# Tokens of the joint experts turned by VectorE in 32x32 blocks, by way of a scratch in memory, instead of by TensorE

## The chip, the cores and the metric

The kernel runs on one core of one Trainium2 chip. The metric is device time in microseconds, the median of several executions. Before the change: 745.49 us, median of 3 runs (743.95 to 746.71).

## What is computed

Two batches of 2048 rows of 512 numbers pass through two layers of attention and mixing and through a quantised layer (the first phase of the kernel), and then through a layer of 16 experts. Each expert picks its 128 best tokens in each batch, takes them through three matrix products and adds the result, weighted, back to those rows:

```python
logits = einsum('bsd,de->bse', x, Wg) + bg
probs = softmax(logits, axis=-2)                     # over the tokens
vals, idx = top_k(transpose(probs, (0, 2, 1)), 128)  # per batch and expert
xe = x[bidx, idx]                                    # 128 rows of 512
h = relu(xe @ w1[e] + b1[e]); h = relu(h @ w2[e] + b2[e])
out = scatter_add(x, idx, (h @ w3[e] + b3[e]) * vals)
```

## The kernel before

The first phase works on 32 tiles of 128 rows and takes the span up to some 418 us. It leaves the normalised rows in memory (`xn4`). Experts 0 to 3 of batch 0 ("early", `tok_e`) are computed while the other experts' tokens are still being chosen, up to some 466 us. The last stage, from about 475 us on, has twelve *joint* experts (e = 0 to 11, for experts 4 to 15), each for both batches at once, and four *single* ones (s = 0 to 3: experts 0 to 3 of batch 1), which are woven into the joint experts 1, 4, 7 and 9 (`SINGLE`). A joint product is made of three passes, since numbers are split into a high part (`_h`) and the rest (`_l`). A single one takes one pass.

How the tokens of a joint expert came to PE: POOL gathers 128 rows of each batch with an indirect DMA (`gather`, `tok`, a token on each partition). PE turns them in eight 128x128 transposes (`tokens`, line 1318) into two PSUM banks, so that the features lie on the partitions: chunk c holds the features 128c to 128c+127. ACT copies the high part to `tokT_h` (`token_hi`), DVE subtracts it from the bank into `tokT_l` (`token_lo`). For a single expert there are four transposes (`single_tokens`, line 361 in `four_transposes`) and a copy by ACT (`single_copy`).

The order of an iteration e on each engine is written out by hand:
- PE: `single_tokens`, `hidden(e, 0)`, `single_first`, `tokens(e + 1)`, `outputs(e - 1)`, `single_second`, `hidden(e, 1)`, `single_outputs` (those of a single expert only where one is woven in).
- ACT: `split_hi(3e + 1)`, `single_copy`, `relu(e, 0, .)` twice, `single_relu`, `token_hi(e + 1)`, `split_hi(3e + 2)`, `single_relu`, `split_hi(3e + 3)`, `relu(e, 1, .)` twice.
- DVE: `split_lo(3e + 1)`, `hidden_lo(e, 0, .)` twice, `token_lo(e + 1)`, `split_lo(3e + 2)`, `weighted(e - 1, 0)`, `split_lo(3e + 3)`, `weighted(e - 1, 1)`, `hidden_lo(e, 1, .)` twice.
- POOL: `gather(e + 2)`, then the adds of e - 1 to the output.
- SP: `load_raw(i)`, 1 MB of weights into one of three buffers, waits until the split of load i - 3 is done. `load_single` brings a single expert's weights, 1 MB each.

Each engine takes its own list in order. A weight passes from `w_raw` through `split_hi` (ACT) and `split_lo` (DVE) before PE uses it. Load 3e - 1 holds the first weights of expert e, 3e + 1 the second, 3e + 3 the third. Line 1973 is the subtraction of all `_lo` steps, line 1496 the copy of all `_hi` steps, line 354 the products in three passes, line 994 and line 1423 those of a single pass. Line 2124 is an operation of the first phase that writes every fourth word (`lg_t`); line 1251 loads every second column of a tile into PE.

Of the kernel before, what the change touches and what calls it, by code (L numbers as in the profile page):

```python
# [35 lines left out]
P = 128  # L36
# [12 lines left out]
def build(nc, io):  # L49
# [36 lines left out]
        p_ev a_ev p_sv a_sv s_gather  # L86
# [12 lines left out]
    sem_tok = [[ctx.enter_context(nc.semaphore(f"tok_in{i}{b}")) for b in range(B)] for i in range(2)]  # L99
# [195 lines left out]
    tok_h, tok_l = place("tokT_h", [P, C, B * P], F32R), place("tokT_l", [P, C, B * P], F32R)  # L295
    tokT_s, h1_s = place("single_tokT", [P, D]), place("single_h1", [P, D])
# [4 lines left out]
    for i in range(RAW, WR):  # L301
        w_h.append(place(f"w_h{i}", [P, C, D], F32R))
    pos = place("pos", [P, TOP], U32)
# [6 lines left out]
    es = place("es", [HEADS, GB])  # L310
    y_s = place("single_y", [P, D])
    bias_s = place("single_bias", [P, FIRST])
    assert top[0] <= at_cd + 16 * KB, (top[0], at_cd + 16 * KB)
# [44 lines left out]
    def four_transposes(pe, bank, src):  # L358

        for c in range(C):  # L360
            last = pe.transpose(bank[:, c * P:(c + 1) * P], src[:, c * P:(c + 1) * P], ident[:, :])  # L361
        return last

# [213 lines left out]
    def _(sp):  # L577
# [48 lines left out]
        def load_early(i):  # L626
# [3 lines left out]
            sp.dma_start(w_e[RING[i % 5]][:, :, :], chunked(io.w[layer][e])).then_inc(sem_early[i % 5], 16)  # L630
# [57 lines left out]
        def load_raw(i):  # L688
# [4 lines left out]
            sp.dma_start(w_raw[i % RAW][:, :, :], chunked(io.w[layer][FIRST + e])).then_inc(sem_raw[i % RAW], 16)  # L693

        def load_single(s, layer):
# [4 lines left out]
            else:  # L700
                at, was = divmod(i - 4, 3)
                sp.wait_ge(sm.p_sv, 4 * at + was + 2)
            sp.dma_start(w_e[i % 4][:, :, :], chunked(io.w[layer][s])).then_inc(sem_early[i % 4], 16)
# [39 lines left out]
    def _(pe):  # L743
# [240 lines left out]
        def early_tokens(e):  # L984
# [3 lines left out]
            four_transposes(pe, bank, tok_e[e]).then_inc(sm.p_ev, 1)  # L988
# [318 lines left out]
        def tokens(e):  # L1307
            for b in range(B):
                pe.wait_ge(sem_tok[e % 2][b], 16 * (e // 2 + 1))
                if e == 0:  # L1310
                    pe.wait_ge(sm.k_pos, 2)
                else:
                    pe.wait_ge(sm.d_tlo, B * (e - 1) + b + 2)
                    if b == 1 and e - 1 in SINGLE:
                        pe.wait_ge(sm.a_sv, 4 * SINGLE[e - 1] + 1)
                for c in range(C):
                    bank = token_bank(e, b, c)
                    last = pe.transpose(bank[:, c * P:(c + 1) * P], tok[e % 2][:, b, c * P:(c + 1) * P], ident[:, :])  # L1318
                last.then_inc(sm.p_tok, 1)

        def hidden(e, layer):
# [3 lines left out]
            if layer == 0:  # L1325
                pe.wait_ge(sm.d_tlo, 2 if e == 0 else B * (e + 1) + 1)
# [4 lines left out]
            for pair in range(2):  # L1331
# [3 lines left out]
                if layer == 1 and e in SINGLE:  # L1335
                    pe.wait_ge(sm.a_sv, 4 * SINGLE[e] + 2 + pair)
# [40 lines left out]
        def outputs(e):  # L1377
# [3 lines left out]
            for b in range(B):  # L1381
# [3 lines left out]
                if b == 1 and e in SINGLE:  # L1385
                    pe.wait_ge(sm.a_sv, 4 * SINGLE[e] + 4)
# [10 lines left out]
        def single_tokens(s, u):  # L1397

            pe.wait_ge(sm.s_gather, 16 * (s + 1))
            pe.wait_ge(sm.d_tlo, B * u + 3)  # L1400
            four_transposes(pe, ps_tok[1], tok_s).then_inc(sm.p_sv, 1)

        def single_first(s, u):
# [3 lines left out]
            pe.wait_ge(sm.a_sv, 4 * s + 1)  # L1407
            early_layer(ps_hid[2], w, tokT_s, range(C)).then_inc(sm.p_sv, 1)

        def single_second(s, u):  # L1410
# [3 lines left out]
            pe.wait_ge(sm.a_sv, 4 * s + 2)  # L1414
            early_layer(ps_hid[3], w, h1_s, range(C)).then_inc(sm.p_sv, 1)

        def single_outputs(s, u):
# [3 lines left out]
            pe.wait_ge(sm.a_sv, 4 * s + 3)  # L1421
# [40 lines left out]
        tokens(0)  # L1462
        keep_warm(3, wh, ps_y[0])
        for e in range(JOINT):
            if e in SINGLE:
                single_tokens(SINGLE[e], e)
# [3 lines left out]
            if e + 1 < JOINT:  # L1470
                tokens(e + 1)
# [14 lines left out]
    def _(act):  # L1486
# [1451 lines left out]
```

## Time and profile before

| | |
|---|---|
| median of 3 runs | 745.49 us (743.95 to 746.71) |
| span of the profiled execution | 743.2 us |
| PE, busy | 716.2 us (96%) |
| DVE, busy | 521.6 us (70%) |
| ACT, busy | 401.9 us (54%) |
| POOL, busy | 420.4 us (57%) |
| chain that ended last | PE 84%, issue 6%, DMA 4%, DVE 3% |
| moved by DMA | 118.04 MB, mean 159 GB/s |

The profile is of one execution. The span runs from its first to its last instruction, and the measured time is 2.3 us longer. PE is TensorE's products and PEld its weight loads, DVE is VectorE, ACT ScalarE, POOL GpSimd, and SP the engine that issues most of the DMAs. The chain is the work that ended last, followed back from the last instruction to what released each step. The joint stage is the part from 475 to 734 us.

### The profile page before, as it was taken

Reading aid. Unit: us, or ns where it says so; the run is one execution under the profiler, and the core shown is the slowest. Engines: PE = TensorE matmul, PEld = TensorE weight load, DVE = VectorE, ACT = ScalarE, POOL = GpSimd, SP = SyncE. Lnnn points to the kernel's source line nnn. Section 1 sums busy time; section 2 is a strip of 40 time slices with the busy share of each in tenths; the row PEclk is TensorE's granted clock in tenths of the full one; section 3 lists DMA queues with packets and bytes.
Section 4 is the critical chain, followed back from the end, with each engine's and each line's share of the span. In section 5 each row is a group of like instructions: output and inputs, shape, how many; then the busy total and the mean of one; then the engine's idle time right before and its main releaser. Section 6 shows DMA issues by size and latency. Waiting matters only on the chain.

```text
span 743.2 us, 12766 instructions
## 1 busy us (share of the span) xinstructions
PE 716.2 (96%) x4513; PEld 624.9 (84%) x4513; DVE 521.6 (70%) x978; ACT 401.9 (54%) x680; POOL 420.4 (57%) x621
## 2 busy tenths in 40 slices
PE   6999999999999999999999799999999999999994
PEld 5765888888888888888888778798999899899894
DVE  5786789889888888876896697464663565463561
ACT  5755444444544545868668334364664656464641
POOL 2825788888888887786788622503521443340132
PEclk9999999999999999999999899999999999999998
DMA  9610121221222213111117898696796698895534
GB/s 317 256 30 15 43 86 62 88 86 58 88 79 82 71 58 108 52 60 44 49 45 264 322 396 279 149 391 186 222 370 185 185 330 293 289 266 167 142 86 58
DMA packets 61671, 118.04 MB, mean 159 GB/s; under 512 B 6056, under 2 KB 7464, under 8 KB 61608
## 3 DMA queue, kind: packets, MB, share of 16 engines
q1 hardware_dynamic: 54312, 100.44, 38.7%
q0 software_dynamic: 7296, 16.78, 10.3%
q8 instruction: 37, 0.61, 0.3%
q14 instruction: 26, 0.21, 0.1%
HBM read 91.76 MB, written 25.21 MB: 157 GB/s over the span
## 4 chain that ended last, share of the span: by engine, by line
PE 84%; issue 6%; DMA 4%; DVE 3%; ACT 2%; POOL 1%; POOLq 0%; SPq 0%; DVEq 0%; ACTq 0%
PE bank L354 39%; PE banks L354 9%; PE bank L361 6%; PE bank L994 6%; PE banks L861 4%; PE banks L867 4%; DMA out<-y,ids 3%; PE banks L871 2%; PE banks L994 2%; PE banks L872 2%; PE banks L1423 1%; PE banks L1028 1%; PE bank L1318 1%; PE bank L1041 1%; DMA out<-x 1%
## 5 line engine op out<-in xcount | busy, mean ns | idle before, releaser
L2844 POOL DMA_INDIRECT out<-y,ids x24 | 46.1, 1922 | 157.4 <-DVE y L2555 155.5
L1973 DVE TENSOR_TENSOR w_l<-w_raw,w_h 128x2048 fp32r<-128x2048 f32 x35 | 80.1, 2291 | 63.2 <-ACT w_h L1496 49.4
L1961 DVE BATCH_NORM_STATS2 bn<-x 128x6 f32<-128x512 f32 x113 | 77.7, 688 | 8.2 <-DMA x<-x 5.4
L1496 ACT ACTIVATE w_h<-w_raw 128x2048 fp32r<-128x2048 f32 x36 | 68.5, 1918 | 7.2 <-DMA w_raw<-w 7.2
L1892 ACT ACTIVATE h<-bank,b 128x512 f32<-128x512 f32 x48 | 33.0, 688 | 62.5 <-PE bank L354 57.8
L1973 DVE TENSOR_TENSOR hT_l<-h,hT_h 128x512 fp32r<-128x512 f32 x48 | 33.0, 689 | 39.8 <-ACT hT_h L1898 37.7
L354 PE MATMUL bank<-tokT_h,w_h 128*128 128x256 f32 x188 | 55.1, 293 | 0.0
L2607 POOL TENSOR_SCALAR rstd<-mean_var 128x1 f32<-128x1 f32 x108 | 25.7, 238 | 50.9 <-DVE mean_var L1966 42.6
L354 PE MATMUL bank<-tokT_h,w_l 128*128 128x256 f32 x188 | 53.2, 283 | 0.0
L354 PE MATMUL bank<-tokT_l,w_h 128*128 128x256 f32 x188 | 53.2, 283 | 0.0
L354 PE MATMUL bank<-wf_h,xdT_h 128*128 128x512 f32 x128 | 52.6, 411 | 0.0
L354 PE MATMUL bank<-wf_h,xdT_l 128*128 128x512 f32 x128 | 50.3, 393 | 0.0
L354 PE MATMUL bank<-hT_h,w_h 128*128 128x256 f32 x176 | 50.1, 285 | 0.0
L354 PE MATMUL bank<-wf_l,xdT_h 128*128 128x512 f32 x128 | 50.0, 390 | 0.0
L354 PE MATMUL bank<-hT_l,w_h 128*128 128x256 f32 x176 | 49.8, 283 | 0.0
L354 PE MATMUL bank<-hT_h,w_l 128*128 128x256 f32 x176 | 49.8, 283 | 0.0
L1650 ACT ACTIVATE q<-bank,bq 128x512 f32<-128x512 f32 x32 | 22.0, 688 | 45.0 <-PE bank L354 44.5
L2687 POOL TENSOR_TENSOR x<-x,mix_bias 128x512 f32<-128x512 f32 x32 | 41.3, 1292 | 1.9 <-PE bank L361 1.8
L2625 POOL TENSOR_TENSOR qT_l<-q,qT_h 128x512 fp32r<-128x512 f32 x32 | 41.4, 1295 | 0.7 <-ACT qT_h L1652 0.7
L2723 POOL TENSOR_TENSOR x<-x,ffn_bias 128x512 f32<-128x512 f32 x32 | 41.8, 1305 | 0.0
L1492 ACT ACTIVATE xn<-x,rstd 128x512 f32<-128x512 f32 x32 | 26.1, 816 | 24.4 <-POOL rstd L2622 20.8
L1973 DVE TENSOR_TENSOR xdT_l<-bank,xdT_h 128x512 fp32r<-128x512 f32 x32 | 22.0, 689 | 23.7 <-ACT xdT_h L1496 23.4
(419 smaller groups left out, 2380.1 us busy)
## 6 DMA issues: line engine op xcount, KB each, us to landing
w_raw<-w SPq DMA_DIRECT2D x36, 1024.0 KB
early_w<-w SPq DMA_DIRECT2D x24, 1024.0 KB, 10.0
x<-x SPq DMA_DIRECT2D x32, 256.0 KB, 2.7
out<-x SPq DMA_DIRECT2D x32, 256.0 KB, 2.0
xn<-xn SPq DMA_DIRECT2D x32, 256.0 KB
mask<-mask_t SPq DMA_DIRECT2D x8, 256.0 KB, 3.4
slot_all<-slots SPq DMA_DIRECT2D x4, 512.0 KB, 7.8
stage<-wk SPq DMA_DIRECT2D x1, 1024.0 KB, 7.7
```

The lines of the kernel that those rows point to most:

```text
L354: last = pe.matmul(out, a, b, start=(n == 0), stop=(n == 3 * len(pairs) - 1))
L361: last = pe.transpose(bank[:, c * P:(c + 1) * P], src[:, c * P:(c + 1) * P], ident[:, :])
L861: last = pe.matmul(both_halves[:, a, 0:WIDE], xh[:, d, :], wc_h[:, d, a, :], start=(d == 0), stop=(d == C - 1))
L994: last = pe.matmul(bank[:, c * P:(c + 1) * P], w[:, d, c * P:(c + 1) * P], x[:, d * P:(d + 1) * P], start=(d == 0), stop=(d == C - 1))
L1496: act.activation(dst, src, ACT.Copy).then_inc(sem, 1)
L1892: act.activation(h32[n % 2][:, :], ps_hid[n % 4][:, :], ACT.Relu, bias=bias)
L1961: dve.bn_stats(bn6[which][:, j % 2, :], src[:, :]).then_inc(sem_bn[which], 1)
L1973: dve.tensor_tensor(dst, src, hi_part, ALU.subtract).then_inc(sem, 1)
L2625: pool.tensor_tensor(dst, src, hi_part, ALU.subtract).then_inc(sem, 1)
L2687: pool.tensor_tensor(x2[j % 2][:, :], x2[j % 2][:, :], cbias[:, batch(j), :], ALU.add).then_inc(sm.g_x2b, 1)
L2723: pool.tensor_tensor(x1_of(k)[:, :], x1_of(k)[:, :], fbias[:, :], ALU.add).then_inc(sm.g_x1b, 1)
L2844: pool.indirect_dma_start(out=out_rows, out_offset=bass.IndirectOffsetOnAxis(ap=ids[:, r:r + 1], axis=0), in_=y[e % 2][b][:, :], in_offset ...
```

## The change

The gathered rows of joint experts 1 to 11 and of all single experts are no longer turned by PE. SP stores them to a scratch in memory (`parts`, `single`) in pieces of 128 numbers: the scratch holds first the first quarter of every token, then the second quarter, and so on. SP then loads it back with 512 contiguous numbers to a partition, so that partition 32q + n holds quarter q of the tokens 4n to 4n + 3. DVE transposes this in 32x32 blocks (`turn_blocks`), reading and writing every fourth number. After it, partition p holds the features 4p to 4p + 3, where it held p, 128 + p, 256 + p and 384 + p before. The first layers' weights are loaded to match: "(p c) n" for "(c p) n", which makes four rows of a weight one contiguous run of 8 KB to a partition. The early tokens and those of joint expert 0 are still transposed by PE, reading every fourth column (`four_row_transposes`, `first_tokens`).

`tok_raw`, which the turns write, lies in the place of `tok_l`: a turn waits until `hidden(e - 1, 0)` has ended, and `token_lo` works in place. Both batches' high parts are made by one copy on ACT, and the rests by one subtraction on DVE. The turns stand where `token_lo` stood; `token_hi` and `token_lo` come later in the lists, behind the next weight's split. The store and the load stand on SP behind every third `load_raw`, each with its waits. `gather(e)` on POOL waits for the store of expert e - 2.

```diff
+        def turn_blocks(eng, out, rows):
+            return eng.transpose(out.rearrange("p c (k t) -> p t c k", k=QBLK),
+                                 rows.rearrange("p (t k c) -> p t c k", t=P // QBLK, c=C))
+        def expert_weights(layer, e):
+            w = io.w[layer][e]
+            return w.rearrange("(p c) n -> p c n", c=C) if layer == 0 else chunked(w)
...
+        def store_parts(e):
+            sp.wait_ge(sem_tok[e % 2], 32 * (e // 2) + (32 if e % 2 else 16))
+            if e >= 2:
+                sp.wait_ge(sm.q_in, 16 * (e - 1))
+            for b in range(B):
+                sp.dma_start(io.parts[b].rearrange("(q p f) -> p q f", p=P, f=P),
+                             tok[e % 2][:, b, :].rearrange("p (q f) -> p q f", f=P)).then_inc(sm.q_out, 16)
+        def load_parts(e):
+            sp.wait_ge(sm.q_out, 16 * B * e)
+            if e == 1:
+                sp.wait_ge(sm.k_pos, 2)
+            if e >= 2:
+                sp.wait_ge(sm.d_tr, B * (e - 1))
+            sp.dma_start(tok_parts[:, :, :], io.parts.rearrange("b (p f) -> p b f", p=P)).then_inc(sm.q_in, 16)
...
         for b in range(B):
-            sp.wait_ge(sem_tok[0][b], 16)
+            sp.wait_ge(sem_tok_first[b], 16)
+        store_parts(1)
+        store_single(0)
+        load_parts(1)
+        load_single_parts(0)
         for i in range(RAW + 1, len(order)):
             load_raw(i)
+            e = i // 3 + 1
+            if i % 3 == 1 and e < JOINT:
+                store_parts(e)
+                if e in SINGLE:
+                    store_single(SINGLE[e])
+                load_parts(e)
+                if e in SINGLE:
+                    load_single_parts(SINGLE[e])
...
         for e in range(JOINT):
-            if e in SINGLE:
-                single_tokens(SINGLE[e], e)
             hidden(e, 0)
             if e in SINGLE:
                 single_first(SINGLE[e], e)
-            if e + 1 < JOINT:
-                tokens(e + 1)
...
         def token_hi(e):
-            for b in range(B):
-                act.wait_ge(sm.p_tok, B * e + b + 1)
-                act.wait_ge(sm.p_h, max(0, 4 * (e - 1) + 2))
-                for part in token_parts(e, b):
-                    hi(sm.a_thi, tok_h[:, part, b * P:(b + 1) * P], in4(token_bank(e, b, part.start))[:, part, :])
+
+            act.wait_ge(sm.d_tr, B * e)
+            hi(sm.a_thi, tok_h[:, :, :], tok_raw[:, :, :])
...
+        def turn_tokens(e):
+
+            dve.wait_ge(sm.p_h, 4 * e - 2)
+            for b in range(B):
+                dve.wait_ge(sm.q_in, 16 * e)
+                turn_blocks(dve, tok_raw[:, :, b * P:(b + 1) * P], tok_parts[:, b, :]).then_inc(sm.d_tr, 1)
+        def token_lo(e):
+
+            dve.wait_ge(sm.a_thi, e + 3)
+            lo(sm.d_tlo, tok_l[:, :, :], tok_raw[:, :, :], tok_h[:, :, :])
...
             if e + 1 < JOINT:
-                token_lo(e + 1)
+                turn_tokens(e + 1)
+            if e + 1 in SINGLE:
+                turn_single(SINGLE[e + 1])
             for n in range(2):
                 if nxt < len(order):
                     split_lo(nxt)
                     nxt += 1
                 if e >= 1:
                     weighted(e - 1, n)
+                if n == 0 and e + 1 < JOINT:
+                    token_lo(e + 1)
...
         def gather(e):
-            if e >= 2:
-                pool.wait_ge(sm.p_tok, B * (e - 1))
+            if e == 2:
+                pool.wait_ge(sm.p_tok, B)
+            if e >= 3:
+                pool.wait_ge(sm.q_out, 16 * B * (e - 2))
```

## Rows read from the trace of the kernel before

**Rows 1.** The page: the span, and PE's busy time.

```profile
span 743.2 us, 12766 instructions
PE 716.2 (96%) x4513; PEld 624.9 (84%) x4513; DVE 521.6 (70%) x978; ACT 401.9 (54%) x680; POOL 420.4 (57%) x621
```

**Rows 2.** Busy time by stretches; last columns: granted clock, DMA share, GB/s.

```profile
core 0: us, PE busy (x) PEld busy (x) DVE busy (x) ACT busy (x) POOL busy (x), PEclk, DMA share, GB/s
516.78:534.62 17.84, 17.84 (x131) 16.89 (x130) 11.41 (x10) 10.96 (x12) 9.05 (x5) 1.00 0.76 217
534.62:552.50 17.88, 17.88 (x131) 16.89 (x130) 11.42 (x10) 11.44 (x13) 4.17 (x4) 1.00 1.04 356
415.00:420.00 5.00, 2.21 (x11) 2.22 (x12) 3.43 (x11) 3.88 (x7) 2.77 (x7) 0.60 0.69 268
475.00:706.00 231.00, 230.88 (x1648) 213.24 (x1649) 127.78 (x117) 129.76 (x153) 72.32 (x47) 1.00 0.80 250
```

**Rows 3.** The chain that ended last, in time: start, length, what.

```profile
487.75 0.44 PE bank L361 x4
488.19 5.76 PE bank L354 x48
...
522.54 0.87 PE bank L1318 x8
```

**Rows 4.** Groups of instructions: count, busy us, mean ns, idle before.

```profile
L1973 DVE TENSOR_TENSOR w_l<-w_raw,w_h 128x2048 fp32r<-128x2048 f32 x35 | 80.1, 2291 | 63.2 <-ACT w_h L1496 49.4 <-issue 13.8
L1496 ACT ACTIVATE w_h<-w_raw 128x2048 fp32r<-128x2048 f32 x36 | 68.5, 1918 | 7.2 <-DMA w_raw<-w 7.2
L1973 DVE TENSOR_TENSOR tokT_l<-bank,tokT_h 128x512 fp32r<-128x512 f32 x23 | 14.8, 685 | 15.9 <-ACT tokT_h L1496 15.9
L1496 ACT ACTIVATE tokT_h<-bank 128x512 fp32r<-128x512 f32 x23 | 12.5, 600 | 5.9 <-issue 5.9
L1318 PEld LDWEIGHTS bank<-ident,tok 128*128 128x128 f32 x94 | 10.6, 141 | 0.6 <-DMA tok<-xn,ids 0.5
L1251 PEld LDWEIGHTS bank<-pack,ident 128*64 128x64 f32 x16 | 1.3, 138 | 0.2
```

**Rows 5.** DVE in time: a strided write (L2124) and a dense one.

```profile
362.58 0.27 DVE L2124 TENSOR_TENSOR lg_t<-lg,rstd_all 128x64 f32<-128x64 f32 x1
...
390.30 0.22 DVE L2109 TENSOR_TENSOR lg<-lg,lg_sum 128x64 f32<-128x64 f32 x1
```

**Rows 6.** DVE in time, in the iteration of e=2.

```profile
523.87 0.69 DVE L1973 TENSOR_TENSOR hT_l<-h,hT_h 128x512 fp32r<-128x512 f32 x1 [1.54 <-ACT hT_h L1898]
...
528.86 0.81 DVE L2555 TENSOR_SCALAR y<-banks,b,vals 128x512 f32<-128x512 f32 x1
```

**Rows 7.** DMA: packets, MB, share in 487.75 to 505; in 475 to 706; issues.

```profile
q1 hardware_dynamic: 2799, 5.54, 85.2%
...
q0 software_dynamic: 5279, 12.45, 22.2%
...
x<-x SPq DMA_DIRECT2D x32, 256.0 KB, 2.7
out<-x SPq DMA_DIRECT2D x32, 256.0 KB, 2.0
...
later<-later SPq DMA_DIRECT2D x1, 64.0 KB, 2.2
...
slots<-slot_rows SPq DMA_DIRECT2D x1, 16.0 KB, 1.8
```

**Rows 8.** SP's issues, and ACT, in time, in the iteration of e=3.

```profile
531.94 8.55 SPq L693 DMA_DIRECT2D w_raw<-w  x2
...
547.63 1.91 ACT L1496 ACTIVATE w_h<-w_raw 128x2048 fp32r<-128x2048 f32 x1 [3.17 <-DMA w_raw<-w]
```

**Rows 9.** SP, POOL and DVE in time, at the start of the joint stage.

```profile
446.75 31.21 SPq L693 DMA_DIRECT2D w_raw<-w  x3
...
472.47 0.94 POOL L2833 DMA_INDIRECT tok<-xn,ids  x1 [0.30 <-issue]
...
482.44 0.69 DVE L1973 TENSOR_TENSOR hT_l<-h,hT_h 128x512 fp32r<-128x512 f32 x1 [2.13 <-ACT hT_h L1898]
483.05 1.28 DVE L1973 TENSOR_TENSOR tokT_l<-bank,tokT_h 128x512 fp32r<-128x512 f32 x2
```

More of the change, by code:

```diff
@@ L98, in build @@
     sem_raw = [ctx.enter_context(nc.semaphore(f"raw_in{i}")) for i in range(RAW)]
[L99 removed]
+    sem_tok = [ctx.enter_context(nc.semaphore(f"tok_in{i}")) for i in range(2)]
+    sem_tok_first = (sem_tok[0], ctx.enter_context(nc.semaphore("tok_in_first1")))
     sem_cut = [ctx.enter_context(nc.semaphore(f"cut_in{i}")) for i in range(2)]
@@ L302, in build @@
         w_h.append(place(f"w_h{i}", [P, C, D], F32R))
+    at_parts = top[0]
+    tok_parts = place("tok_parts", [P, B, D], at=at_parts)
     pos = place("pos", [P, TOP], U32)
@@ L362, in four_transposes, with of_chunk, four_row_transposes @@
         return last
+    def of_chunk(rows, c):
+        return rows[:, c::C]
+    def four_row_transposes(pe, bank, rows):
+        for c in range(C):
+            last = pe.transpose(bank[:, c * P:(c + 1) * P], of_chunk(rows, c), ident[:, :])
+        return last
+    def turn_blocks(eng, out, rows):
[4 more added lines that the diff above has]
+        return w.rearrange("(p c) n -> p c n", c=C) if layer == 0 else chunked(w)
     def blocks(t):
@@ L692, in load_raw @@
                 lo_done(sp, i - RAW)
-            sp.dma_start(w_raw[i % RAW][:, :, :], chunked(io.w[layer][FIRST + e])).then_inc(sem_raw[i % RAW], 16)
+            sp.dma_start(w_raw[i % RAW][:, :, :], expert_weights(layer, FIRST + e)).then_inc(sem_raw[i % RAW], 16)
         def load_single(s, layer):
@@ L1304, in _, with first_tokens @@
         pe.transpose(ps[0][:, 0:HEADS], top_v[:, :], ident[0:HEADS, 0:HEADS]).then_inc(sm.k_tr, 1)
-        def tokens(e):
+        def first_tokens():
             for b in range(B):
[L1309 to L1315, printed above, removed]
+                pe.wait_ge(sem_tok_first[b], 16)
+                pe.wait_ge(sm.k_pos, 2)
                 for c in range(C):
-                    bank = token_bank(e, b, c)
-                    last = pe.transpose(bank[:, c * P:(c + 1) * P], tok[e % 2][:, b, c * P:(c + 1) * P], ident[:, :])
+                    bank = token_bank(0, b, c)
+                    last = pe.transpose(bank[:, c * P:(c + 1) * P], of_chunk(tok[0][:, b, :], c), ident[:, :])
                 last.then_inc(sm.p_tok, 1)
@@ L2532, in split_lo, with first_token_lo, turn_single @@
             lo(sm.d_w, w_l[i % WR][:, :, :], w_raw[i % RAW][:, :, :], w_h[i % WR][:, :, :])
-        def token_lo(e):
+        def first_token_lo():
             for b in range(B):
                 t = slice(b * P, (b + 1) * P)
-                for i, part in enumerate(token_parts(e, b)):
-                    dve.wait_ge(sm.a_thi, B * e + b + 1 + (i if e == 0 else 1))
-                    lo(sm.d_tlo, tok_l[:, part, t], in4(token_bank(e, b, part.start))[:, part, :], tok_h[:, part, t])
+                for i, part in enumerate(token_parts(0, b)):
+                    dve.wait_ge(sm.a_thi, b + 1 + i)
+                    lo(sm.d_tlo, tok_l[:, part, t], in4(token_bank(0, b, part.start))[:, part, :], tok_h[:, part, t])
+        def turn_tokens(e):
+            dve.wait_ge(sm.p_h, 4 * e - 2)
+            for b in range(B):
+                dve.wait_ge(sm.q_in, 16 * e)
[3 more added lines that the diff above has]
+            lo(sm.d_tlo, tok_l[:, :, :], tok_raw[:, :, :], tok_h[:, :, :])
+        def turn_single(s):
+            dve.wait_ge(sm.qs_in, 16 * (s + 1))
+            if s >= 1:
+                dve.wait_ge(sm.p_sv, 3 * s - 2)
+            turn_blocks(dve, tokT_s[:, :].rearrange("p (c t) -> p c t", c=C), h1_s[:, :]).then_inc(sm.d_ts, 1)
         def hidden_lo(e, layer, pair):
@@ L2556, in weighted @@
                               ALU.add, ALU.mult).then_inc(sm.d_y, 1)
-        token_lo(0)
+        first_token_lo()
         split_lo(1)
@@ L2574, in _ @@
                     weighted(e - 1, n)
+                if n == 0 and e + 1 < JOINT:
+                    token_lo(e + 1)
             hidden_lo(e, 1, 0)
@@ L2933 @@
     io["cut"] = nc.dram_tensor("cut", (4 * 2048, 1), F32, kind="Internal").ap()
+    io["parts"] = nc.dram_tensor("parts", (2, 128 * 512), F32, kind="Internal").ap()
+    io["single"] = nc.dram_tensor("single", (128 * 512,), F32, kind="Internal").ap()
     io["slots"] = nc.dram_tensor("slots", (4 * 2048,), BF16, kind="Internal").ap()
```

71 lines of the change are left out of this document (39 added, 32 removed).

## The prediction

> **What bounds the kernel now.** I read the page first: TensorE is busy 96% of the span [rows 1]. Then the table of stretches, cut at the starts of the joint experts' first layers: from 475 to 706 us PE is busy for 230.88 of 231 us at clock 1.00, and DVE, ACT and POOL for 55%, 56% and 31% [rows 2]. Then the chain of work that ended last: from 475 to 684 us it is PE without a gap, so a microsecond taken from PE there ends the kernel a microsecond earlier as long as nothing else is late. In that chain stand the transposes that the change removes: 0.87 us for the eight of a joint expert (11 such pieces) and 0.44 us for the four of a single one (4 pieces) [rows 3]. A hidden layer is 5.76 us. The reserve that matters is the DMA engines': mean share 0.80 from 475 to 706, but 1.04 in the iteration of e=3 [rows 2].
>
> **What is removed.** 11 x 0.87 + 4 x 0.44 = 11.3 us of PE, all on the chain. ACT loses two copies of some 0.6 from PSUM for each expert and gains one of 128x1024, half of the 1.92 of a 128x2048 and a little, say 1.0; DVE's two subtractions of 0.69 become one of 128x1024, half of 2.29, 1.2 us [rows 4]. These two changes are even.
>
> **The turns.** New on DVE are two 32x32-block transposes of 128x512 for each expert, one for a single. The trace has none. A DVE pass over 128x512 takes 0.69 [rows 4]. Read and written data here lie 16 bytes apart. Such a write is in the trace: 128x64 with every fourth word takes 0.27 where a dense one takes 0.22 [rows 5], 0.05 for 64 elements, so 0.4 for 512. Bounds: 0.69, and 16 blocks each as an instruction of its own. For the latter, 128x64 at 0.22 bounds a block of 32 columns, call it 0.19: 3.0 us. I take 1.0, the dense pass with most of the strided write, since it is nearest to that row. The Trainium skill, "SBUF — State Buffer", section "Door 1: The DMA port swizzle", says that an access that crosses to another 16-byte line pays a penalty, with fp32 free up to four elements. These turns cross on every access, reading and writing. The row agrees for the write, with 0.05 us in 64. By the rule the read pays as well, 1.4 instead of 1.0 a turn, and the sum would be worse by about 1 us, at the start only.
>
> **Do the turns hide in a plain iteration?** Take e=2, from 516.78. hidden_lo(2, 0, 1) ends 7.8 us after the start, and then came both subtractions [rows 6]. Now: turns to 9.8, split_lo 12.1, weighted (0.81) 12.9, token_lo 14.1. PE wants the tokens at 17.84 - 0.87 = 17.0. Reserve 2.9 us, so no cost; it is gone when a turn takes about 2.5. In a single's iteration there is much more. DVE's sum goes from 11.4 [rows 2] by 2.0 + 1.2 - 1.4 to 13.2 of 17.0.
>
> **PE's strided reads.** The 16 early and 8 first token transposes now load every fourth column. The load of a tile with every second column (L1251) took 138 ns, a dense one 141 [rows 4]. I take nothing; doubled loads would cost 24 x 0.14 = 3.4 us, some on the chain. That is the upper bound.
>
> **The DMAs.** A hardware packet of 2 KB cost 0.852 x 16 x 17.25 / 2799 = 84 ns, so a 1 MB weight load is 2.7 us of all engines [rows 7]. An expert's load of parts is 256 such: 1.3 us. Its store is 1024 packets of 512 B, bounded by a quarter of 84 ns and by 84 ns: 1.3 to 5.4 us. A 64 KB load made of 512 B rows landed in 2.2 us where 16 KB took 1.8 [rows 7], so a packet is near the lower end; I take 27 ns, 1.7 us. Together 3.1 for an expert and 1.5 for a single: 11 x 3.1 + 4 x 1.5 = 40 us of DMA, on top of 0.80 x 231 = 185. Until the weights end that is 225 of some 223 us: full on average, though the share can go to 1.05. The first layers' weights come with 8 KB runs instead of 2 KB; the bytes are the same and no such load is in the trace; I take nothing, and a tenth of 14 such loads, 4 us of DMA either way, as bounds.
>
> **The waits on SP.** SP now stands at the store until the gather has landed, and at load_parts until the store has. Behind it stand load_raw(3k+5), load_single and load_raw(3k+6), and behind those ACT's splits. The store joins a hardware queue behind weights already issued. How long that queue gets: load_raw(12) issued at 531.94 and split at 547.63, after 3.17 us of waiting [rows 8]. POOL's transfers take 0.222 x 231 / 46 = 1.1 us of all engines each [rows 7]; four loads, two adds and two gathers make 4 x 2.7 + 4 x 1.1 = 15.2 of these 15.7 us, so the queue works in order and is full. Now for k=2, from its start T: load 10 at T+5; store done at T+12.4; load_parts, then load 11 at T+13.4 instead of T+12.1; singles; load 12 at T+17; the load of parts in front. Load 12 then lands some 32 us after T, 15 after the start of e=3, ACT's split ends at 16.8 and relu(3, 1, 0) at 18.1. PE wants it at 17.0 + 5.8 = 22.8. So 4 to 5 us of reserve, no cost. The same holds at k=5; at k=7 the long iteration drains the queue. POOL's gather(e) now waits for the store of e-2 instead of its transposes; the stores are done before POOL comes to it, except at the start.
>
> **The start.** Here nothing is ahead. The second gather of expert 5 was issued at 472.47, and I let it land at 476.2. Two stores issued to 477.2, done at 480.5 (1.7 of data, 1.3 fixed, which is an out store's 2.0 less 0.7 of data, and 0.3 beside an early add); load_parts 480.5 to 484.0 (1.3 of data, 2.0 fixed, which is an x load's 2.7 less 0.7, and its issue), load_single_parts 484.6 [rows 7]. Before, DVE ended hidden_lo at 483.13 and subtracted at once [rows 9]. Now: two turns to 486.0, turn_single 487.0, split_lo(2) 489.3, token_lo(1) 490.5. hidden(1, 0) began at 488.19 [rows 3] and now begins at 490.6: 2.4 us later, though PE is free at 487.5. A PE idle of 3 us could lower the clock: after 5 us without work it was granted 0.60 in 415 to 420 [rows 2]. That would add up to 2 us; I leave it to the range. SP then issues load_raw(4) at 481.5 (477.96 before) [rows 9], and load_single(0, 0) at 489.3, since load_parts(2) waits for a store behind load_raw(4), landing about 495, before PE wants it at 496.4.
>
> **Sum.** +2.4 at the start of e=1. From there ten token pieces and three single ones fall away: -8.7 - 1.3. Net -7.6 at the end of the stage. The last expert and its adds are as before. The span of the profiled execution is 743.2 [rows 1], the median 745.49, so 2.3 lie around it: 743.2 - 7.6 + 2.3 = 737.9.
>
> **Rivals.**
> A, all hidden: the parts arrive as early as the old transposes and hidden(1, 0) starts at 487.5. Then 11.3 less 0.6 (DVE's hidden_lo ends at 483.13 and PE must wait for it without the eight transposes): 745.5 - 10.7 = 734.8. Against it: the start's four steps in a row.
> B, slower side: the DMA engines become the bound. Each store followed by its load on SP empties the hardware queue for the fixed time of 1.3 to 2.0 us [rows 7]. With 225 us of work in 223 and 10 such gaps of 2 us, 22 us are too much. Load 12 has 5 us of reserve and a single's long iteration gives some back, say 12 in all, so some 10 us come out as PE stalls at e=4, 7 and 9: 737.9 + 10 = 748. It decides once load 12 lands more than 5 us later than above, that is with 512 B packets above some 45 ns or with gaps in every iteration. For it: share 1.04 [rows 2] and the wait [rows 8]. Against it: in most iterations SP waits for a split anyway.
> C, also slower: a turn costs 3.0. Token_lo ends at 18.1 in a plain iteration instead of 17.0, 7 times 1.1, and the start is later by 6: 737.9 + 7.7 + 6 = 752.
> D, no effect: the freed PE time goes to another wait of the same size, such as single_outputs on weighted: 745.5. Against it: PE has no idle in the stage now, and no removed transpose stands between single_second and single_outputs.
>
> **Chances.** Forecast 0.52, A 0.10, B 0.21, C 0.07, D 0.10. The range takes A and B with the store's and the clock's bounds: 734 to 748.5. The likeliest case's own range is 735 to 741.5. A measurement tells 0.5% (3.7 us) from no change. Faster than 741.8: forecast, A: 0.62. Within: D, half of B: 0.21. Slower than 749.2: C and the worse half of B: 0.17.
>
> **What would show it.** PE records of L1318 only 8, of L361 on single tiles none. A PE gap of about 3 us near 488, ending with token_lo. Transposes on DVE near 1.0. Share of the DMA engines above 0.9 from 490 to 690. ACT waiting for w_raw near e=3 and 6, with no PE gap behind it; a PE gap at single_first or single_outputs speaks for B, at hidden(e, 0) in plain iterations for C.

## The result, and the profile after

The changed kernel takes 754.33 us, median of 4 runs (751.87 to 754.78), where the kernel before takes 745.63 (4 runs, 743.95 to 746.71): ratio 1.0115, 95% interval 1.0095 to 1.0135. It is slower by 1.15%, and outside the range forecast (734 to 748.5), where the forecast was 737.9, faster.

From the page of the changed kernel (span; engines; shares of the chain that ended last):

```profile
span 752.8 us, 12590 instructions
PE 712.1 (95%) x4409; PEld 618.1 (82%) x4409; DVE 544.7 (72%) x993; ACT 399.4 (53%) x665; POOL 425.4 (57%) x621
...
PE 65%; DMA 14%; issue 11%; DVE 5%; ACT 2%; POOL 2%; SPq 1%; POOLq 0%; DVEq 0%; ACTq 0%
```

The 104 matmuls are gone (4513 to 4409 [rows 1]), but PE's busy time fell by 4.1 us and not by 11.3, and PE is 65% of the chain instead of 84%; DMA is 14% of it instead of 4%. The table of stretches tells why (columns as in [rows 2]):

```profile
475.00:706.00 231.00, 216.42 (x1484) 196.62 (x1485) 141.46 (x123) 119.76 (x131) 76.52 (x46) 0.97 0.93 300
...
488.00:492.00 4.00, 0.00 (x0) 0.00 (x0) 3.92 (x3) 4.00 (x5) 0.00 (x0) 0.88 0.97 321
492.00:496.00 4.00, 3.23 (x15) 3.26 (x16) 4.00 (x5) 2.86 (x3) 0.00 (x0) 0.50 0.40 110
...
584.00:588.00 4.00, 2.38 (x4) 1.13 (x5) 2.72 (x4) 0.48 (x1) 1.98 (x3) 0.82 0.89 251
588.00:592.00 4.00, 4.00 (x15) 2.26 (x14) 0.00 (x0) 0.97 (x2) 2.81 (x3) 0.75 1.03 311
```

Between 475 and 706 us PE now stands idle for 14.6 us (0.12 before), and the mean clock is 0.97. PE idles in three places only; the timeline of PE names them (in brackets the idle time and what ended it):

```profile
483.13 0.39 PE L1428 MATMUL bank<-hT_h,w_h 128*128 128x256 f32 x1 [0.65 <-DVE hT_l L2025]
492.77 0.55 PE L359 MATMUL bank<-tokT_h,w_h 128*128 128x256 f32 x1 [5.07 <-DVE tokT_l L2025]
...
580.08 0.36 PE L359 MATMUL bank<-hT_h,w_h 128*128 128x256 f32 x1 [1.91 <-ACT single_h L1962]
585.62 5.37 PE L1482 MATMUL banks<-early_w,single_h 128*128 128x512 f32 x8 [2.45 <-issue]
...
648.22 0.36 PE L359 MATMUL bank<-hT_h,w_h 128*128 128x256 f32 x1 [2.01 <-ACT single_h L1962]
653.76 2.69 PE L1482 MATMUL banks<-early_w,single_h 128*128 128x512 f32 x4 [2.44 <-issue]
```

**The account.** At the start: 0.65 + 5.07 idle, and then `hidden(1, 0)` takes 8.21 us (chain, below) instead of 5.76, since the clock was granted at 0.50, the lower of its two levels, in 492 to 496: 8.2 us in all. In e=4: 1.91 + 2.45 idle, and `single_outputs` takes 5.37 instead of 3.67 (its length where the clock is full, as in the experiment with 2 KB runs): 6.1 us. The same in e=7: 6.1 us. Together 20.4 against 11.3 saved, +9.1; PE's last product ends 9.8 us later than before, so 0.7 are not assigned. (`hidden(0, 0)` begins at 475.06 where it began at 475.12, so these 9.8 us all arise in the joint stage.) No iteration between has a gap, and e=9 has none.

The first chain of the changed kernel, at the start (start, length, what):

```profile
476.56 4.67 DMA parts<-tok
...
482.61 5.45 DMA single_h<-single
...
488.08 1.16 DVE single_tokT L381
489.24 2.14 DVE w_l L2025
491.38 1.15 DVE tokT_l L2025
...
492.77 8.21 PE bank L359 x48
```

Store, load, turn, split and subtraction stand in a row, and in the row forecast; what was wrong is their length. And the second, which ends in e=4:

```profile
543.89 11.05 DMA tok<-xn,ids
...
555.37 8.94 DMA parts<-tok
...
565.29 11.19 DMA w_raw<-w
...
576.50 0.03 ACT w_h L1551
...
578.32 0.96 ACT tokT_h L1551
579.28 0.66 ACT single_h L1962
...
580.08 3.10 PE bank L359 x24
583.17 2.45 issue
585.62 5.37 PE banks L1482 x8
```

Read from below. `single_outputs` (585.62) waits for `weighted(3, 1)` on DVE, which ends at 585.5; it stands in DVE's list behind two weight splits, and the first of them began only at 578.45, after 8.02 us of waiting for ACT's split of the same weight:

```profile
584.71 0.81 DVE L2626 TENSOR_SCALAR y<-banks,b,vals 128x512 f32<-128x512 f32 x1
```

And `hidden(4, 1)` waits for a single expert's hidden values (`single_h`) on ACT. ACT makes them at 579.3 because in its list `split_hi(14)` stands ahead, and this weight landed at 576.5. It landed so late since SP issued it at 565.29, behind `load_parts(5)`, which waits for the store of expert 5, 9 us long; and the store had waited for its gather, 11 us long. So SP stood still twice. The timelines of SP and ACT show the same (from 475 to 740 us ACT waited twice for a weight before, 6.8 us in all, the longest 3.6; now eight times, 44.7 us, the longest 9.6):

```profile
554.96 0.92 SPq L736 DMA_DIRECT2D parts<-tok  x2
564.33 0.36 SPq L746 DMA_DIRECT2D tok_parts<-parts  x1
...
565.29 2.39 SPq L718 DMA_DIRECT2D w_raw<-w  x3
...
576.50 1.91 ACT L1551 ACTIVATE w_h<-w_raw 128x2048 fp32r<-128x2048 f32 x1 [8.71 <-DMA w_raw<-w]
...
ACT w_h L1551 <- DMA w_raw<-w: 44.7, 8, 9.6
```

### The profile page after: what moved, and what is told of

It reads as the page before. It is cut to its first block, busy times and chain, and to the rows that moved or that the text cites. A ratio compares the mean times of both kernels' runs of the same rounds, so it can differ in the third digit from the quotient of the medians.

```text
span 752.8 us, 12590 instructions
## 1 busy us (share of the span) xinstructions
PE 712.1 (95%) x4409; PEld 618.1 (82%) x4409; DVE 544.7 (72%) x993; ACT 399.4 (53%) x665; POOL 425.4 (57%) x621
## 2 busy tenths in 40 slices
DMA packets 71286, 131.66 MB, mean 175 GB/s; under 512 B 6712, under 2 KB 21432, under 8 KB 68664
## 4 chain that ended last, share of the span: by engine, by line
PE 65%; DMA 14%; issue 11%; DVE 5%; ACT 2%; POOL 2%; SPq 1%; POOLq 0%; DVEq 0%; ACTq 0%
PE bank L359 31%; PE bank L366 6%; PE banks L359 5%; PE banks L931 4%; PE banks L937 3%; DMA parts<-tok 3%; DMA w_raw<-w 3%; PE bank L1064 3%; DMA out<-y,ids 3%; DMA tok<-xn,ids 3%; PE banks L941 2%; PE banks L1482 2%; PE banks L942 2%; PE banks L1064 1%; DVE w_l L2025 1%
## 5 line engine op out<-in xcount | busy, mean ns | idle before, releaser
L2921 POOL DMA_INDIRECT out<-y,ids x24 | 48.9, 2036 | 153.8 <-DVE y L2626 152.8
L1551 ACT ACTIVATE w_h<-w_raw 128x2048 fp32r<-128x2048 f32 x36 | 68.8, 1911 | 44.7 <-DMA w_raw<-w 44.7
L359 PEld LDWEIGHTS bank<-tokT_h,w_h 128*128 128x128 f32 x188 | 37.2, 198 | 6.2 <-issue 6.2
```

The lines of the kernel that those rows point to most:

```text
L359: last = pe.matmul(out, a, b, start=(n == 0), stop=(n == 3 * len(pairs) - 1))
L1551: act.activation(dst, src, ACT.Copy).then_inc(sem, 1)
L2921: pool.indirect_dma_start(out=out_rows, out_offset=bass.IndirectOffsetOnAxis(ap=ids[:, r:r + 1], axis=0), in_=y[e % 2][b][:, :], in_offset ...
```

## The experiments

Every run is given as its median, its ratio to the kernel before on the same chip, and the 95% interval. In the profiled executions `hidden(0, 0)`, the start of the joint stage, begins anywhere from 472.6 to 475.9 us, though hardly anything ahead of it differs; so I also compare the stage itself, from there to the end of PE's last product: 258.8 us before, 268.6 in the changed kernel. Three runs (22 products, the single expert's turn behind `token_lo`, every turn twice) were made on another chip than the kernels with which they are compared; the kernel before took 745.0 us there and 745.2 here. My theory W was now: SP's two waits (for the gather and for the store) delay the weights, and the start pays for its chain. Against it: D, the DMA engines are simply full, so that any kernel with this traffic is late; and S, the new 8 KB runs of the first weights are slow.

**The waits without the store's result, then without either.** The first takes the load's wait for the store away, by reading rows that have long been in memory; the second also stores a tile that is always there, so SP doesn't wait for the gather either.

```diff
-            sp.wait_ge(sm.q_out, 16 * B * e)
-            sp.dma_start(tok_parts[:, :, :], io.parts.rearrange("b (p f) -> p b f", p=P))...
+            sp.dma_start(tok_parts[:, :, :], io.xn4[0:B * P, :].rearrange("(b p) f -> p b f", b=B))...
```

> The changed kernel, but load_parts and load_single_parts read fixed rows of xn4 (the same bytes in the same 2 KB pieces), so SP no longer stands there until the store has landed. Left out: the experts then work on wrong tokens. The stores stay, and SP still waits for the gather before a store. Theory W (SP stands at these waits, the weight loads behind it are issued late, and PE waits for them at e=4 and e=7): the start shortens from a gap of 5.1 us and 2.4 us at half clock to a gap of about 2, since the parts are there when DVE is free, and most of the 6 us at each of e=4 and e=7 go: 754.3 - 5.5 - 6 to 12 = 737 to 743. Theory D (the DMA engines cannot carry the extra 12 MB, whoever waits): the traffic is the same, so the 12 us at e=4 and e=7 stay: about 749.

> As the run before, and the stores send a constant tile, so SP waits neither for the gather nor for the store: all the extra traffic, none of the waits of SP on it. Left out: the same as in the run before. Theory W: no gaps at e=4 and e=7, 736 to 739, and faster than the run before by as much as the gather's wait costs. Theory D: 12 us of gaps stay, about 749.

Measured: 740.60 us, 0.9938 (0.9921 to 0.9955), and 737.66 us, 0.9908 (0.9885 to 0.9932). Both move the same 131.66 MB as the changed kernel. The traffic of the second, by stretch (DMA share and GB/s at the end), is denser than the changed kernel's (0.92, 298 from 475 to 700); below it the same stretch of the first:

```profile
475.00:700.00 225.00, 221.49 (x1558) 203.40 (x1558) 150.89 (x130) 129.56 (x140) 83.75 (x47) 1.00 0.95 317
```

```profile
475.00:700.00 225.00, 220.02 (x1530) 202.13 (x1529) 147.05 (x128) 125.40 (x137) 83.34 (x47) 0.98 0.95 315
```

PE's gaps at e=4 and e=7 are gone in both. D falls: the engines carry this traffic at 317 GB/s without a stall. Without the wait for the store the kernel is 13.7 us faster; without the wait for the gather 2.9 more, and these lie at the start (a gap of 4.33 us and a `hidden(1, 0)` of 8.51 in the first; gaps of 1.54 and 1.98, and 5.99, in the second). The total of the first lay in its range, but not for all the reasons expected: the start was to shorten to a gap of about 2 us, and it hardly did. The second stands at the 737.9 of the forecast, and for the forecast's reasons: the transposes saved, a start some 2 us late, no cost from SP (its joint stage is 7.4 us shorter than before, forecast 7.6; this profile is of the fastest of its four runs, 735.1). So most of what the forecast lacked is the price of SP's waits.

**2 KB runs.** The joint experts' first weights are loaded in two DMAs of every second row, which makes runs of 2 KB again.

```diff
-            sp.dma_start(w_raw[i % RAW][:, :, :], expert_weights(layer, FIRST + e))...
+            for part in ((slice(0, C, 2), slice(1, C, 2)) if i % RAW == 2 else (slice(0, C),)):
+                sp.dma_start(w_raw[i % RAW][:, part, :], expert_weights(layer, FIRST + e)[:, part, :])...
```

> The changed kernel with the joint experts' first weights loaded in two transfers of every second row, so that a run is 2 KB again and not 8 KB; the result is the same. Theory S (packets of 8 KB hold back the software queue, so the gather of expert 9 lands 11 us after its issue and all behind it is late): the gather lands in about 5 us, the gaps at e=4 and e=7 fall by half or more, 745 to 749. If the size of a run does nothing: 754 within 2.

Measured: 752.24 us, 1.0103 (1.0086 to 1.0119), an interval that overlaps the changed kernel's; the joint stage is 0.6 us shorter, 268.0. S falls: the gather of expert 5 landed after 9.8 us, not 5, and the store after it took 9.9. The gaps stand where they stood (1.01 + 2.43 in e=4, 3.43 + 0.94 in e=7, and 1.03 and 1.19 elsewhere), with 1.5 us of lower clock in `hidden(7, 1)` instead of `single_outputs`.

**Expert 1 and the first single expert turned by PE, as before.** The diff puts `second_tokens` and `first_single_tokens` on PE, and starts the stores with expert 2.

```diff
-        store_parts(1)
-        store_single(0)
-        load_parts(1)
-        load_single_parts(0)
...
         for e in range(JOINT):
+            if e == 1:
+                first_single_tokens()
             hidden(e, 0)
+            if e == 0:
+                second_tokens()
```

> The changed kernel, but joint expert 1 and single expert 0 are still transposed by PE, as before the change; the scratch serves from joint expert 2 on. The start costs 5.1 us of gap, 0.7 of another and 2.4 of low clock in the changed kernel. Theory: these go and 1.3 us of transposes come back, so 754.3 - 7 = 747.3, with the gaps at e=4 and e=7 as they are. If the lateness at e=4 comes from the late start (the queue of loads that is already behind at e=1), it goes too: about 741.

Measured: 747.58 us, 1.0040 (1.0025 to 1.0055). The total falls by 6.7 us, with 1.3 us of PE given back, so about 8.1 gross where the account says 8.2. Part of this agreement is chance: the profile also has less idle time at e=4 and e=7, and gaps of 1.47 and 0.48 us and 1.5 us of lower clock in `hidden(7, 1)` that the changed kernel doesn't have. The gaps at e=4 (0.84 + 2.45, and 5.37 us of `single_outputs`) and e=7 (2.03 + 0.93) remain, so the two losses are separate.

**The load one weight later, with each start.** Only the place of `load_parts` and `load_single_parts` on SP changes: behind the next `load_raw`.

```diff
             if i % 3 == 1 and e < JOINT:
                 store_parts(e)
                 if e in SINGLE:
                     store_single(SINGLE[e])
+            if i % 3 == 2 and (i + 1) // 3 < JOINT:
+                e = (i + 1) // 3
                 load_parts(e)
```

> The changed kernel with one move in SP's order: the loads of an expert's quarters (and of a single token's) stand one weight load later than their stores, so that SP passes its wait for the store with the next weights already issued. In the changed kernel SP waited for the store of expert 5 from 555.4 to 564.3 us and issued the weights behind it at 565.3, which landed at 576.5. Theory W (the wait for the store, one expert's weights late, is what stops PE at e=4 and e=7): those weights go out some 9 us earlier, the four gaps of 1.91, 2.44, 2.01 and 2.44 us vanish, and with them the 1.7 us of single_outputs at the lower clock, twice: 754.3 - 8.8 - 3.4 = 742. The start is untouched. Theory L (the chain gather, store, load, turn is itself too long for an iteration of 18 us): the parts of expert 5 now land some 10 us later, VectorE's turn waits for them, and with it its splits; the gaps go to hidden(e,0): 752 to 757. Theory G (it is the wait for the gather, ahead of the store, which this kernel keeps): about half of the gain, 748.

> Both cures at once: expert 1 and the first single token are turned by PE as before the change, and the later loads go one weight load behind their stores. With expert 1 by PE the kernel took 747.6 us, with gaps of 0.84 and 2.45 us and 1.7 us of lower clock at e=4 and of 2.03 and 0.93 us at e=7. Theory W: these go, 747.6 - 6.2 - 1.7 = 739.7. Theory L: the gaps move to hidden(e,0), 747 to 751.

Measured: 741.62 us, 0.9956 (0.9940 to 0.9973), and with the old start 734.60 us, 0.9866 (0.9848 to 0.9883). The gaps at e=4 and e=7 are gone with either start, and here the stores and loads carry the true rows, so L and G fall too: the chain is not too long, and the wait for the gather, which both keep, costs nothing there by itself. SP's timeline in the second:

```profile
563.17 0.92 SPq L736 DMA_DIRECT2D parts<-tok  x2
565.67 0.34 SPq L718 DMA_DIRECT2D w_raw<-w  x1
568.74 0.36 SPq L746 DMA_DIRECT2D tok_parts<-parts  x1
...
475.00:706.00 231.00, 231.00 (x1642) 213.30 (x1641) 154.20 (x134) 134.35 (x147) 82.34 (x49) 1.00 0.96 309
```

The last line is its table of stretches: PE has no idle time at all, at full clock, with the DMA engines at 0.96. The weight is issued while the store is still on its way, and ACT waits for weights 12.6 us instead of 44.7. PE ends its work at 723.36, 10.5 us before the kernel before. Of these 0.6 lie ahead of the joint stage; the stage is 9.9 us shorter, and that is the PE work removed, ten token pieces of 0.87 and three of 0.44, 10.0. This version is faster than both kernels, by 1.3% than the one before. I had expected 739.7 and not 734.6: with it went the gaps of 1.47 and 0.48 us and the 1.5 us of lower clock named above, 3.4 of these 5.1 us, where I had added up only the gaps at e=4 and e=7; another 0.6 lies ahead of the stage, and 1.1 is not assigned.

**Stores and loads on ACT's queue.** On top of the old start.

```diff
             relu(e, 0, 0)
+            if 1 <= e < JOINT - 1:
+                load_parts(e + 1)
...
             relu(e, 1, 1)
+            if e + 2 < JOINT:
+                store_parts(e + 2)
```

> As the kernel with expert 1 turned by PE (747.6 us), and the stores and loads of the quarters are issued on ACT's queue instead of SP's: the store of expert e+2 behind the last relu of expert e, the load of expert e+1 behind the first relu of expert e, each where what it waits for has landed long before. SP then waits for no token. Theory W: SP issues its weights as before the change, the gaps at e=4 and e=7 go: 747.6 - 6.2 - 1.7 = 739.7, and a little less if ACT's queue takes the parts' packets out of the order of the weights, 737 to 740; faster than the kernel before. Rival (ACT is the late engine in these iterations and pays for the issues, some 0.1 to 0.4 us each for 3 or 4 of them an iteration, or waits for a gather that took 11 us): 742 to 748.

Measured: 775.93 us, 1.0434 (1.0392 to 1.0476), much slower, and outside both ranges expected. The chain of the profiled execution (769.0 us) says what I had overlooked:

```profile
512.59 10.98 DMA parts<-tok
...
523.58 7.77 DMA tok_parts<-parts
...
531.45 2.19 DVE tokT_raw L381 x2
...
542.58 9.91 DMA tok_parts<-parts
```

SP no longer waits (ACT's wait for weights is down to 0.4 us), but the load for expert e + 1 is now issued only in iteration e, in which DVE has to turn it, and takes 8 to 10 us. So DVE waits for parts 35.0 us in nine times, ACT waits 36.2 us for DVE's turns, and PE stands for 2.9 to 4.9 us at each of five `hidden(e, 0)`, four times for a `relu` that ACT reaches late. ACT's queue also stood for the store itself, twice, 13.0 us. Two things follow. The store takes 11 us on a queue of its own too (512.59 to 523.56): what makes it slow is not, or not only, its place behind weights in SP's queue, as I had thought. (Both queues use the same 16 DMA engines, SP's 51.7% of their time from 475 to 706 us and ACT's 14.8%; whether the weights delay the store there, no run shows.) And the place of the load in the order matters as much as the wait that goes with it.

**The idle time and the clock.** Products of the identity with itself fill the start's gap on PE: 15 on the changed kernel, then 22 on the one with later loads.

```diff
         for e in range(JOINT):
+            if e == 1:
+                for _ in range(15):
+                    pe.matmul(ps_y[0][:, 0:P], ident[:, :], ident[:, :], start=True, stop=True)
             hidden(e, 0)
```

> The changed kernel with 15 products of the identity by itself (128x128, about 0.28 us each, 4.2 us) put on PE ahead of hidden(1,0), where it stood idle for 5.07 us and then took 8.21 us for work that took 5.8 us before. Their result is overwritten. Theory C (the slow hidden(1,0) is the clock, which was granted at half after the idle time): PE is busy in the gap, hidden(1,0) takes 5.8 to 6.2 us, the total is 2.2 us shorter, 752.1. Rival (hidden(1,0) is slow for another reason, its operands arriving piece by piece from ACT and DVE): it takes 8.2 us again and the total is the same, 754.3.

> On top of the later loads (741.6 us), 22 products of the identity by itself ahead of hidden(1,0), 0.234 us apart, 5.1 of the 5.44 us in which PE stood idle there. 15 of them left 1.95 us idle, and hidden(1,0) still took 7.47 us with a granted clock below 1. Theory C (the clock falls for the idle time): with the gap all but full hidden(1,0) takes 5.8 us, 2.3 us less, 739.3. Rival (the products of the identity are not what keeps the clock, or the slow product has another cause): 741.6.

Measured: 751.65 us, 1.0091 (1.0065 to 1.0118), against 754.33; and 739.44 us, 0.9927 (0.9911 to 0.9944), against 741.62. The chains, with 15 products first, then with 22 (L1528 are the products of the identity, two records for each):

```profile
493.83 7.48 PE bank L359 x48
```

```profile
487.49 4.91 PE banks L1528 x44
492.40 5.76 PE bank L359 x48
```

Fifteen left 1.95 us idle, and `hidden(1, 0)` still ran partly at the lower clock (7.48, 0.7 less than without them). The total fell by 2.7, with runs from 747.6 to 755.8. The 2 us beyond that 0.7 are not from the start: in this profile e=4 (0.83 + 2.44 idle) and e=7 (3.45 + 1.03, and 1.4 of lower clock in `hidden(7, 1)`) cost 9.2 us instead of 12.2, though nothing there was changed; with 0.5 at the start that is the 3.5 us by which its joint stage is shorter (265.1). So the price of e=4 and e=7 differs from one execution to another, and this run alone settles nothing. Twenty-two left nothing, and it takes 5.76: 2.2 us off the total, as expected. So at the start the fall of the clock comes from the idle time, and is worth 2.2 to 2.4 us on top of it.

**The single expert's turn behind `token_lo`,** on the version with later loads.

```diff
-            if e + 1 in SINGLE:
-                turn_single(SINGLE[e + 1])
             for n in range(2):
...
                 if n == 0 and e + 1 < JOINT:
                     token_lo(e + 1)
+                if n == 0 and e + 1 in SINGLE:
+                    turn_single(SINGLE[e + 1])
```

> On top of the later loads (741.6 us), VectorE turns a single token's block behind token_lo instead of ahead of the weights' split and token_lo. At the start the single's turn held VectorE for 1.10 us on the way to token_lo(1), which hidden(1,0) waits for. Theory Q (everything queued ahead of token_lo at the start is paid in full): hidden(1,0) begins 1.0 us earlier, 740.6. Rival: the clock's drop behind the gap is shorter or longer with the gap, so up to 2 us more, 738.6, or nothing: 741.6.

Measured: 740.89 us, 0.9944 (0.9928 to 0.9961), 0.7 us less than without it, which the intervals do not part. In the traces the way from the turns' start to `hidden(1, 0)` is 491.26 - 484.62 = 6.6 us before the edit and 491.08 - 485.44 = 5.6 with it: the 1.0 us is there, but in the profiled execution the parts had landed 0.8 later. DVE's turns with the edit:

```profile
485.44 2.11 DVE L381 STREAM_TRANSPOSE tokT_raw<-tok_parts 128x512 f32<-128x512 f32 x2 [3.88 <-DMA tok_parts<-parts]
```

**Every turn twice,** on the fastest version.

```diff
+                turn_blocks(dve, tok_raw[:, :, b * P:(b + 1) * P], tok_parts[:, b, :]).then_inc(sm.d_tr, 1)
+                dve.wait_ge(sm.d_tr, 2 * B * (e - 2) + 2 * b + 1)
                 turn_blocks(dve, tok_raw[:, :, b * P:(b + 1) * P], tok_parts[:, b, :]).then_inc(sm.d_tr, 1)
```

> On top of the version with expert 1 turned by PE and the later loads (734.6 us), VectorE turns every block of tokens twice, each time waiting for the first: 18 turns of 1.1 us and the wait more, 2.3 to 2.6 us for each of 9 experts. Theory H (VectorE has more slack than that in an iteration of 17 to 22 us, the turn is hidden): 734.6 to 736. Rival (the turn lies on the way from the parts' landing to hidden(e,0), as the price of 3 us in the forecast supposed): up to 2.4 us for each of 9 experts, 745 to 756.

Measured: 742.10 us, 0.9948 (0.9927 to 0.9970): 7.5 us for some 20 us more on DVE. Neither expectation holds. From PE's timeline:

```profile
514.79 5.37 PE L1493 MATMUL banks<-early_w,single_h 128*128 128x512 f32 x8 [2.05 <-issue]
...
617.33 0.36 PE L359 MATMUL bank<-tokT_h,w_h 128*128 128x256 f32 x1 [0.42 <-DVE tokT_l L2051]
```

PE waits 0.4 to 0.5 us for `token_lo` behind e=3, e=6 and e=8, the plain iterations in which DVE also turns a single expert's tokens; behind the other plain ones it doesn't wait. 2.05 go at the first `single_outputs`, which waits for `weighted`, with 1.7 at the lower clock, and 0.8 in two smaller gaps. So each turn, done once, is hidden. With 2.2 us more for the two turns the reserve is overdrawn by some 0.4 where a single's turn stands with them, so it is about 1.8 us there, and at least 2.2 elsewhere.

## Why the prediction was wrong, point by point

**What bounds the kernel, and what is removed: right.** PE is the bound where nothing else is late. The fastest version shows the removed transposes almost to the number (10.0 of records, 9.9 in the joint stage).

**The turns: right.** Forecast 1.0, bounds 0.69 to 3.0. All 26 in the changed kernel (DVE by form: least, median, most):

```profile
L381 DVE STREAM_TRANSPOSE tokT_raw<-tok_parts x22: 1067/1116/1155, 485.7 to 712.6; 128x512 f32<-128x512 f32 x22
L381 DVE STREAM_TRANSPOSE single_tokT<-single_h x4: 1107/1115/1158, 488.1 to 668.8; 128x512 f32<-128x512 f32 x4
```

The 1.4 us that would have followed from a penalty on both sides did not come; 0.12 of the 0.4 did. Rival C had no ground. The reserve of 2.9, gone at a turn of 2.5, was worked out for e=2, and there two turns of 2.2 us still fitted. It is smaller, about 1.8, in e=3, 6 and 8, where a single's turn comes on top, which the step left out.

**PE's strided reads: wrong, and small.** I took nothing, from a load of every second column. Loads of every fourth column (PEld by form, changed kernel):

```profile
L376 PEld LDWEIGHTS bank<-ident,early_tok x12: 197/212/230, 407.2 to 438.7; 128*128 128x128 f32 x12
L1383 PEld LDWEIGHTS bank<-ident,tok x6: 197/204/217, 472.2 to 473.4; 128*128 128x128 f32 x6
```

The same loads took 139 and 141 before, dense. So a step of 16 bytes costs 65 to 70 ns, half again. My step had also misread its row: the load of every second column has 64 columns, and I set it against a dense one of 128. Dense loads of 64 stand in the kernel before too, and are shorter:

```profile
L1251 PEld LDWEIGHTS bank<-pack,ident x16: 136/138/139, 449.8 to 456.6; 128*64 128x64 f32 x16
L911 PEld LDWEIGHTS bank<-ident,lg_t x7: 108/110/112, 140.1 to 397.8; 128*64 128x64 f32 x7
```

So 138 against 141 was no sign that a step of 8 bytes is free; 138 against 110 may in part come from the different products around these loads, so its price isn't shown either. The 24 loads of every fourth column are 1.7 us more of PEld, and nothing of it is seen in the total: `hidden(0, 0)` begins at 475.06 (475.12 before). The Trainium skill, "SBUF — State Buffer", section "Door 1: The DMA port swizzle", says that a run of accesses is at full rate only with two or more in a 16-byte line. The loads with one in a line agree, 204 and 212 ns against 139 and 141. For two in a line no run here shows it.

**The DMAs' sum: right.** The share is 0.92 to 0.96, and the traffic can be carried with PE never idle (the fastest version: 0.96, 309 GB/s). The price of a store's packet was right as well: in 476 to 482 SP's queue moved the stores' packets of 512 B and hardly anything else, 0.448 x 16 x 6000 / 1573 = 27 ns each (the rows stand below), forecast 27. What I did not see is that at such a share a transfer takes long, even one of 256 KB.

**The waits on SP: here the prediction failed.** The step said: "Load 12 then lands some 32 us after T", that is 15 after the start of e=3, with 4 to 5 us of reserve, and "The same holds at k=5; at k=7 the long iteration drains the queue." I walked only one store, that of expert 4. For it the step held, though just: with T at 522.39 load 12 was split at 558.88, 36.5 after T instead of 32, and PE had no gap. The next store, k=3 for expert 5, I did not walk. Its gather is issued by POOL at 543.89, behind two adds, the first of which had waited 5.9 us for DVE, and lands at 554.9; its store 8.9 later; load 14 goes out at 565.3 and lands 11.2 later. None of the three has a term like it in the step: a gather was let land in 3.7 us (at the start), and SP was taken to find it landed. And the step's last sentence was the wrong way round: it counted the iteration with a single expert as the one that gives time back, since PE is longer busy there. But in that iteration `single_relu` and `token_hi` stand behind `split_hi(3e + 2)` in ACT's list, and PE wanted `single_relu` at 578.17, long before it came to load 14 itself, with `hidden(5, 0)` at 590.99. Two gaps of 1.9 and 2.4 us follow, and the lower clock. At k=6, for expert 8, the same happens: the store goes out at 619.75, the load of the parts at 631.21 and the weight at 632.18, and PE stands in e=7.

**The start: right in kind, wrong in size.** Forecast 2.4 us later, measured 4.6 (492.77 against 488.19), and 2.4 more for the clock, which I had left to the range. The terms, forecast and measured: end of the stores 480.5 and 481.2; the parts loaded and the first turn begun 484.0 and 485.7; the single's quarter landed 484.6 and 488.06, a load of 256 KB that was issued at 482.61, 1.4 us behind the load of parts, and took 5.45 us, where I had let it land 0.6 behind the parts; split and `token_lo` 490.5 and 492.5. Each transfer was priced in a stretch without neighbours [rows 7], and here the DMA engines were busy for 0.99 of 476 to 482 and 0.96 of 482 to 488. The neighbours were not weights at first, but POOL's gathers and its add, over half of the engines' time (packets, MB, share in 476 to 482: POOL's queue, then SP's, which held the stores):

```profile
q0 software_dynamic: 299, 0.78, 54.7%
q1 hardware_dynamic: 1573, 0.78, 44.8%
```

SP had issued no weight since 447.6; the next one went out at 483.04, behind the single's load.

**Sum.** 737.9 + 12.2 (e=4 and e=7) + 2.2 (start) + 2.4 (clock) = 754.7; measured 754.3. The 12.2 are of one execution; the profile with fifteen products has 9.2 in these places, and the one with 2 KB runs 11.5 behind the start, so the closeness of the sum is in part chance.

**The rivals.** B came nearest: it named the order store, wait, load on SP and PE stalls at e=4, 7 and 9 for 10 us. The places e=4 and 7 are right, the price was 12.2; the DMA engines as the bound, the other half of B, is refuted. The sign named in the forecast, a PE gap at single_outputs for B, pointed the right way. A gave 734.8, and the kernel takes 734.6 when both faults are removed; but that kernel keeps 1.3 us of the transposes on PE that A removes, and had 0.6 us less ahead of the joint stage, so the number agrees in part by chance.

## What to carry to other kernels

A wait on the engine that issues the DMAs delays everything behind it in its list: put the load that waits for a store at least one independent load later, and walk every such store, not one, through the list of the engine that consumes what is queued behind. Price a transfer in the stretch in which it will run: at a DMA share of 0.9 and more a store, a load or a gather of 256 to 512 KB took 4 to 11 us, where loads and stores of 256 KB in the first phase, where the share was 0.20 (100 to 380 us, the kernel before), took 2.0 to 2.7 [rows 7]. Look for the first waiter in each consumer's order, for the delayed item may be needed by another engine's list long before its own use.

## What was unexpected of the hardware

- A store of 512 KB (four quarters of each of 256 rows) took 8.9 us in SP's queue, with weights in it, and 11.0 us in ACT's, with none in that queue. Why it is no faster in a queue of its own stays open.
- PE's clock was granted at 0.50 in 492 to 496 after 5.07 us without work, and the 48 products took 8.21 us instead of 5.76; after 1.95 us without work, 7.48. With the gap filled they took 5.76. But the idle time alone doesn't tell: a gap of 2.43 to 2.45 us ahead of the first late `single_outputs` (e=4) was followed by 5.37 us for its 8 products in two profiles (the changed kernel, expert 1 by PE) and by 3.67, full clock, in two others (the 2 KB runs, the fifteen products).
- A load of a 128x128 f32 tile into PE took 139 to 141 ns dense and 204 to 212 with a step of 16 bytes (the same loads, before and after the change).
